# A fused attention and feed-forward kernel: the projection's first half and the feed-forward tile change places in the TensorE order of a step

## The reference, cut to what matters

```python
xn = _layernorm(x)                       # x: (4, 1024, 1024)
q, k, v = xn @ Wq.T, xn @ Wk.T, xn @ Wv.T   # 16 query heads, 4 key/value heads of 64
att = softmax(where(mask, q k^T / 8, -inf))  # causal, window 512, 4 sink keys
s = (att v) @ Wo.T
# feed-forward on the last row of each of the 4 sequences, 4 rounds:
thought = layer_norm(xn)[:, -1, :] @ agg_w + agg_b
for _ in range(4):
    t = gelu(layer_norm(thought) @ d1_w + d1_b)     # 1024 -> 4096
    thought = thought + (t @ d2_w + d2_b)           # 4096 -> 1024
g = silu(layer_norm(xn + sigmoid(xn @ gate_w + gate_b) * (thought @ bc_w + bc_b)))
x = x + s * g
```

## Time and profile before

| | |
|---|---|
| median of 3 runs | 2451.33 us (2449.65 to 2454.17) |
| the profiled execution | 2447.99 us |
| its span, first to last instruction | 2446.3 us |
| mean granted TensorE clock | 0.956 |
| PE busy | 2248.7 us (92%) |
| PEld busy (weight loads) | 1655.2 us (68%) |
| DVE busy | 1496.4 us (61%) |
| ACT busy | 884.4 us (36%) |

### The profile page before, as it was taken

One profiled execution on the slowest core, in us unless ns is written; L12 is line 12 of the kernel. 1 busy time (PEld: TensorE's weight loads), 2 busy tenths in 40 slices (PEclk: granted clock), 3 DMA queues, 4 the chain that ended last, 5 costly groups with the idle time before them and its releaser, 6 DMA issues. The chain is left out here.

```text
span 2446.3 us, 35525 instructions
## 1 busy us (share of the span) xinstructions
PE 2248.7 (92%) x13576; PEld 1655.2 (68%) x13576; DVE 1496.4 (61%) x3084; ACT 884.4 (36%) x1842; POOL 143.6 (6%) x352
## 2 busy tenths in 40 slices
PE   3779999779999969999987999996899999999998
PEld 2556666567666647666656666663688888888887
DVE  3536666665666654666665566663576666766666
ACT  2215555523555532555552355552311111111111
POOL 1100000010000011000001000000011010111000
PEclk6889999999999989999998999997799999999999
DMA  8664444564334454454355534433634433344331
GB/s 311 240 189 166 156 162 139 179 178 158 133 127 168 171 179 140 169 168 146 132 195 162 174 126 143 168 135 120 230 126 137 137 118 112 130 137 129 131 116 63
DMA packets 164667, 379.08 MB, mean 155 GB/s; under 512 B 18648, under 2 KB 100632, under 8 KB 148656
## 3 DMA queue, kind: packets, MB, share of 16 engines
q1 hardware_dynamic: 157680, 354.06, 42.9%
q0 software_dynamic: 5120, 16.85, 1.9%
q10 hardware_dynamic: 1728, 6.29, 0.7%
HBM read 297.37 MB, written 79.72 MB: 154 GB/s over the span
## 5 line engine op out<-in xcount | busy, mean ns | idle before, releaser
L591 ACT ACTIVATE pt<-t_ps 128x512 f32<-128x512 f32 x480 | 266.5, 596 | 496.3 <-PE t_ps L788 493.4
L988 DVE CUSTOM_DVE_ANT_0 probs<-s_ps,mask 128x644 f32<-128x644 f32 (+5 forms) x512 | 317.2, 656 | 95.6 <-PE s_ps L761 92.7
L600 ACT ACTIVATE probs<-probs,neg_max 128x644 f32<-128x644 f32 (+5 forms) x512 | 352.9, 694 | 21.2 <-DVE neg_max L988 21.2
L710 PE MATMUL j_ps<-x_hi,w 128*128 128x512 f32 x960 | 320.4, 405 | 16.0 <-DMA w<-WT 16.0
L788 PE MATMUL t_ps<-ident,probs 128*128 128x128 f32 x1920 | 273.9, 282 | 7.2 <-ACT pt L591 4.2
L1332 PE MATMUL out_ps<-wo,by_hi 128*128 128x512 f32 x1024 | 273.7, 389 | 0.0
L761 PEld LDWEIGHTS s_ps<-k_hi,q 64*128 64x128 f32 x1536 | 145.4, 184 | 170.2 <-DVE neg_max L988 77.1
L761 PE MATMUL s_ps<-k_hi,q 64*128 64x512 f32 (+4 forms) x1536 | 242.1, 351 | 4.2 <-DVE neg_max L988 4.2
L788 PEld LDWEIGHTS t_ps<-ident,probs 128*128 128x128 f32 x1920 | 212.0, 142 | 48.6 <-issue 15.5
L812 PE MATMUL o_ps<-pt,v 128*64 128x256 f32 x1920 | 235.5, 386 | 0.0
L1005 DVE TENSOR_SCALAR probs<-probs,inv_sum 128x644 f32<-128x644 f32 (+5 forms) x512 | 217.9, 468 | 9.1
(11 more groups left out here) (153 smaller groups left out, 2973.2 us busy)
## 6 DMA issues: line engine op xcount, KB each, us to landing
fw<-in_L_ffn_d_w_dram SPq DMA_DIRECT2D x128, 1024.0 KB, 5.0
w<-WT SPq DMA_DIRECT2D x40, 1024.0 KB, 5.1
probs<-in_L_attn_x_dram POOLq DMA_DIRECT2D x32, 512.0 KB, 5.6
XS<-x_hi SPq DMA_DIRECT2D x32, 512.0 KB, 4.4
XS<-x_lo SPq DMA_DIRECT2D x32, 512.0 KB, 6.2
Y<-y SPq DMA_DIRECT2D x128, 128.0 KB, 1.8
b_x<-in_L_attn_x_dram SPq DMA_DIRECT2D x32, 512.0 KB, 4.2
b_y<-Y SPq DMA_DIRECT2D x32, 512.0 KB, 6.4
```

Of the source, the lines that this page charges most:

```text
L591: act.activation(pt[:, m % PT_SLOTS, :, :], bank[:, :].rearrange("p (h q) -> p h q", q=P), ACT.Copy).then_inc(pt_ready, 1)
L600: act.activation(probs[:, slot, 0:width], probs[:, slot, 0:width], ACT.Exp, bias=neg_max[:, slot:slot + 1], scale=-1.0, accum_out=row_sum[ ...
L710: last = pe.matmul(out[:, :], weights[:, wp * C + c * P:wp * C + c * P + P], xs[:, c, bass.ts(ch, BANK)], start=i == 0, stop=i == STEPS - 1)
L988: dve.tensor_tensor_reduce(out=probs[:, slot, 0:width], in0=s_ps[head % 2][:, 0:width], in1=m, scale=-SCALE, scalar=-NEG, op0=ALU.add, op1 ...
```

## The change

In steps with a share of the projection (0 to 27 of each sequence) the first half of the share moves to between the two pairs of scores, where the feed-forward tile was, and the feed-forward tile moves to between turns 2 and 3 and the last turns. Steps 28 to 31 keep their order. On VectorE `add_sums` moves, in the same steps, behind the masks of heads 2 and 3. No instruction is added or removed.

```diff
                     turn_two(0)
                     if s in HIDDEN_AT:
                         turn_hidden(b, s, HIDDEN_AT[s])
-                    ffn_step(b, s)
+                    if fill:
+                        piece, a, z = fill
+                        q_proj(b, piece, a, (a + z) // 2)
+                    else:
+                        ffn_step(b, s)
                     scores(b, s, 1)
                     turn_two(2)
                     if fill:
-                        piece, a, z = fill
-                        q_proj(b, piece, a, (a + z) // 2)
+                        ffn_step(b, s)
                     turn_two(4)
                     if fill:
                         q_proj(b, piece, (a + z) // 2, z)
@@
                     mask_scores(b, s, 1)
-                    if TILES_AT[s]:
+                    if TILES_AT[s] and not piece_at(s):
                         add_sums(b, s)
                     mask_scores(b, s, 2)
                     mask_scores(b, s, 3)
+                    if TILES_AT[s] and piece_at(s):
+                        add_sums(b, s)
```

## The result

| | before | after |
|---|---|---|
| median | 2449.65 us of 5 runs | 2463.86 us of 5 runs |
| lowest to highest | 2444.54 to 2454.17 | 2461.49 to 2467.45 |
| span of the profiled execution | 2446.3 us | 2459.8 us |

The ratio after to before is 1.0057, 95% interval 1.0039 to 1.0075: slower by 14.2 us in the medians. The forecast was +14.7 us (2466.0, range 2457 to 2476).

The account below looks back on a forecast made before the run. The prediction took TensorE, almost without idle time in steps 0 to 27, as the bound. Its terms summed to 3.67 us a sequence, 14.7 for four, on 2451.33: 2466.0 us, range 2457 to 2476.

Parts of the forecast that it names:

- A full engine: Steps 0 to 27: TensorE busy 258.77 of 260.19 us at clock 1.00, with no hole before the second scores.
- The rival that took the 77.1 us for lost time: Weight loads' mask waits before the second scores were real and the projection covers them: 2389 us, chance 0.03.
- The price of a neighbour: TensorE's matmuls cost by what they follow: leaving the projection for another tiling 0.10 us more, transposes after another tiling 0.06.
- every ordinary kind of step: Per sequence: ten steps with five or six turns +1.60 us, seven with three or four +1.47, eight with one or two +0.16.
- The steps with one or two turns: Eight steps (qb 1 and 2): projection cut +0.21, tile's neighbours -0.18, about +0.02 us each, 0.16 a sequence.
- The rival of equal neighbours: All neighbours cost the same, so only steps 0, 8 and 16 count: +1.8 us, 2453.1, chance 0.08.
- The unseen pair: Tile followed by turns or projection, not shown in the old loop: taken as 0.99 us, bounds 0.10 lower or higher.
- Step 0: No turns; the projection waits for the low part of piece 1, which the tile had covered: +0.79 us a sequence.
- Step 8: The projection hides the tile's 0.36 us wait for VectorE's hidden rows; with +0.16 for neighbours, -0.20 us a sequence.
- Step 16: No tile; second scores' 0.61 us wait hidden, 0.45 returns as turn 4 waits for ScalarE's copy: about -0.15 a sequence.
- The thin cover: add_sums behind two masks costs nothing; divisions finish about 0.2 us before the next turns, tightest in steps with one turn.
- The rival of a late VectorE: add_sums delays the divisions, losing 0.5 us in five steps a sequence: +10 us, 2476, chance 0.07.

Follow-up runs that it names:

- Experiment 3: Changed kernel with the projection's first half put back behind turns 2 and 3, so only the tile moves and add_sums stays late: 2529.55 us, ratio 1.0325.
- experiment 4: Changed kernel with the tile directly behind the second scores and the projection's second half cut around any last turns: 2449.22 us, ratio 0.9995 to the kernel before.
- experiment 5: Kernel before, with the last two projection matmuls moved into the middle of the values in 23 steps of each sequence: 2489.61 us, ratio 1.0156.
- experiment 8: experiment 4 with step 0 in the old order and, in ten steps with five or six turns, tile and second scores after the last turns: 2459.23 us, ratio 1.0036.
- experiment 10: experiment 9 with the five-tiling order of experiment 8 in steps 6, 14 and 22 alone: 2445.62 us, ratio 0.998 to the kernel before.
- experiment 9: experiment 4 with step 0 of each sequence in the order of the kernel before: 2447.10 us, ratio 0.9987 to the kernel before.
- Experiment 2: Changed kernel with add_sums put back ahead of the masks of heads 2 and 3, TensorE in the changed order: 2489.34 us, ratio 1.0156 to the kernel before.
- experiment 6: Kernel before, reordered in steps 0 to 27 except 8 and 16: tile behind first scores, second scores after last turns, one tiling change fewer: 2604.44 us, ratio 1.062.
- experiment 7: experiment 6, but steps with qb 1 and 2 keep the order of the kernel before: 2534.02 us, ratio 1.0338 to the kernel before.
- experiment 1: Kernel before with only add_sums moved behind the masks of heads 2 and 3, TensorE in the old order: 2451.88 us, ratio 0.9999.

## Why the prediction was right

**A full engine.** The reading that TensorE had no hole before the second scores held. Experiment 3 opened that hole and cost 80 us; the change closed nothing. The change itself is the plainest test. The weight loads' wait for the masks fell from the 77.1 us of the earlier trace rows to 10.1, and the run became 14 us longer:
```profile
PEld s_ps L761 <- DVE neg_max L991: 10.1, 12, 0.8
```
The rival that took the 77.1 us for lost time is out.

**The price of a neighbour.** The table above agrees with the forecast within 0.04 us for every ordinary kind of step. These steps make up 3.0 us of the 3.50 of a sequence; the rest is steps 0, 8 and 16. That their cost is the extra change of tiling, and neither the place of the projection nor that of `add_sums`, is shown from three sides: experiment 4 takes the extra change away and 2.8 of these 3.0 us with it; experiment 5 adds two and each step grows by 0.35; experiments 8 and 10 take one more away and the step shrinks by 0.14 to 0.15. The steps with one or two turns have six changes of tiling in both orders, and they did not grow (7.90 and 7.88 in step 2). The rival of equal neighbours is out with these. The unseen pair, tile and then turns, measured 0.99 and stood at neither end of its bounds. That this 0.99 holds the price of a change can be read in step 17, where two tiles follow one another with no change between them:
```profile
342.38 1.92 PE L661 MATMUL o_ps<-fw,cols 128*32 128x512 f32 x16
344.23 0.50 PE L710 MATMUL j_ps<-x_lo,w 128*128 128x512 f32 x1
```
From start to start the two take 1.85 us, where two single tiles take 2 x 0.99 = 1.98. So having a change at both ends of each costs 0.13 more. The Trainium skill, "TensorEngine Tiling (Array Packing)", section Key Properties, says that a change of tiling mode drains TensorE, and the trace agrees.

**The pieces that are waits.** Step 0 lost 0.73 with step 1, forecast 0.81. The trace has the wait for the low part in the open, 0.93, and experiment 9 got the time back by putting the tile there again. Step 8 saved 0.18 of a forecast 0.20. Step 16 was mis-sized most, 0.07 for 0.15: the wait of 0.61 went, but more than I had allowed came back as the wait for ScalarE's copies. Turns 2 to 5 take 1.93 there until the projection. Before, with half of the projection between them, they took 0.84 + 0.46 = 1.30, so 0.63 came back where the prediction had 0.45.

**The thin cover.** `add_sums` behind the masks had about 0.2 us of room in the steps with one turn. After the change the divisions of step 1 end where the turns of step 2 find them:
```profile
186.94 0.69 DVE L1054 TENSOR_TENSOR rows<-o_ps,rows 128x512 f32<-128x512 f32 x1 [0.24 <-PE o_ps L661]
...
188.46 0.62 DVE L1008 TENSOR_SCALAR probs<-probs,inv_sum 128x256 f32<-128x256 f32 x2
```
They end at 188.46 + 0.62 = 189.08 and the turns start at 189.46 with no wait, so the room was 0.38. The rival of a late VectorE did not come true, here or in any other step of the loop: the trace shows no wait of the turns for the divisions in steps 0 to 27. Experiment 2 shows that it was near: with the sums ahead of the masks the same turns waited 0.48.

The sum was 3.67 for a sequence and measured 3.50; with four sequences 14.7 against 13.9 from the trace and 14.2 from the medians. No kind of step missed its term by more than 0.08 a sequence, so the number owes little to errors that cancel.

## What to carry to other kernels

When one engine is full and at its full clock, reordering its work pays only through what each neighbour costs the next; count the changes of TensorE's tiling in a step, and put work of an odd tiling where the tiling changes anyway. A weight load's idle time is no loss by itself; look for idle matmuls, or for start-to-start lengths above their usual value. When an instruction group is moved later, list everything that waits behind it on the other engines, the copies that free its buffer too: experiments 6 and 7 lost 155 and 85 us, 107.8 and 60.0 of them in waits for one such copy.

## What the runs showed of the hardware

A pair of changes of tiling around two matmuls costs 0.35 us at the full clock (experiment 5). About 0.1 of a single change lies between the last start of the group ahead and the first start behind it: 213.98 to 214.30 is 0.32 in experiment 5, and two projection matmuls stand 0.23 apart. The rest is the first matmul behind the change: 0.06 for a transpose, 0.12 for a projection matmul (215.31 to 215.66 is 0.35 in experiment 5).

The granted clock can fall within a loop that is almost full. In experiment 5 it was 0.76 over 253 to 260 us, with TensorE busy for 6.64 of the 7.00, and in experiment 2 0.89 over 740 to 755, both times in a step that has the hidden rows' sixteen-column matmuls and a wait near them. The profiles of experiments 1 and 8 have one such fall, in step 8 of one sequence. It is not bound to these steps: experiment 3 has it in step 0 of three sequences, and experiment 6, with waits of 1.2 to 1.8 us in most steps, in steps 2, 4, 10, 18 and others. A fall made its step about 1.6 us longer in experiments 1, 2 and 3. In the kernels before and after, and in experiments 4, 9 and 10, the clock was 1.00 in all of these loops, though step 8 of the kernel before has the same matmuls and a wait of 0.36. What sets it off was not tried and stays open.
